# Attention and a 4-bit dense layer on one core: first queries in head order, and the second half's pieces of x split in the first stage

## The reference

```python
h = x + xattn(layernorm(x), ctx, ctx, pos, mask, Wq, Wk, Wv, Wo)   # x, ctx: (8, 256, 1024)
y = h + ffn(layernorm(h), qweight, qzeros, scales, bias)

def xattn(query, key, value, ...):    # 32 query heads, 8 key/value heads, head size 128
    q, k, v = heads(query @ Wq), heads(key @ Wk), heads(value @ Wv)
    q, k = rope(q), rope(k)           # q * cos + rotate_half(q) * sin
    scores = q k^T / sqrt(128);  where(mask == 0) -> -1e9
    return (softmax(scores) @ v) @ Wo

def ffn(x, ...):
    return x @ (scales * (w4 - zeros)) + bias   # w4: 4-bit values, 1024 x 1024
```

## Time and profile before

| | |
|---|---|
| Median of 3 runs | 2415.59 us (2408.92 to 2416.83) |
| Profiled execution, its own time | 2418.64 us |
| Its span, first to last instruction | 2416.8 us |
| Mean granted TensorE clock | 0.991 |
| PE busy | 2353.0 us, 97% |
| DVE, ACT, POOL busy | 1336.1, 1114.9, 1180.8 us |
| DMA | 346.65 MB, mean 143 GB/s |

### The profile page before, as it was taken

One profiled execution on the slowest core, in us unless ns is written; L12 is line 12 of the kernel. 1 busy time (PEld: TensorE's weight loads), 2 busy tenths in 40 slices (PEclk: granted clock), 3 DMA queues, 4 the chain that ended last, 5 costly groups with the idle time before them and its releaser, 6 DMA issues.

```text
span 2416.8 us, 33647 instructions
## 1 busy us (share of the span) xinstructions
PE 2353.0 (97%) x11552; PEld 1975.2 (82%) x11552; DVE 1336.1 (55%) x1949; ACT 1114.9 (46%) x2515; POOL 1180.8 (49%) x926
## 2 busy tenths in 40 slices
PE   8999998999999999899999999989999999999999
PEld 6887877888888888688888888868887877878887
DVE  4762554666666666666666666637743233343532
ACT  3222123667676667666766667643332222322010
POOL 1410535555665665556665566555664344355110
PEclk9999999999999999999999999999999999999999
DMA  7676674333434335343343333368554454443111
GB/s 262 237 178 223 233 246 152 92 102 100 113 103 114 105 106 155 113 127 102 93 117 106 106 112 103 111 212 284 202 191 168 149 178 166 143 177 113 44 44 53
DMA packets 201241, 346.65 MB, mean 143 GB/s; under 512 B 17744, under 2 KB 126544, under 8 KB 201168
## 3 DMA queue, kind: packets, MB, share of 16 engines
q1 hardware_dynamic: 187088, 310.06, 41.0%
q10 hardware_dynamic: 13312, 33.56, 4.2%
q0 software_dynamic: 768, 2.10, 0.3%
HBM read 238.69 MB, written 106.97 MB: 143 GB/s over the span
## 4 chain that ended last, share of the span: by engine, by line
PE 81%; DVE 7%; DMA 5%; ACT 3%; POOL 3%; issue 1%; SPq 1%; ACTq 0%; DVEq 0%; POOLq 0%
PE ps L208 18%; PE ps L209 18%; PE ps L210 18%; PE ps L690 7%; PE ps L691 7%; PE ps L692 7%; PE ps L622 4%; DMA scores<-in_ctx 2%; DVE rows L1226 1%; DMA xc_scratch<-xring 1%; DMA wraw<-in_L_xattn_Wo 1%; DMA xring<-in_x_tiles 1%; POOL s_buf L1322 1%; ACT probs L864 1%; PE ps L714 1%
## 5 line engine op out<-in xcount | busy, mean ns | idle before, releaser
L208 PE MATMUL ps<-act_t,wq_t 128*128 128x512 f32 x1280 | 512.5, 400 | 20.8 <-DVE act_t L1076 10.9
L210 PE MATMUL ps<-act_t,wq_t 128*128 128x512 f32 x1280 | 501.8, 392 | 0.0
L209 PE MATMUL ps<-act_t,wq_t 128*128 128x512 f32 x1280 | 501.6, 392 | 0.0
L690 PE MATMUL ps<-b_parts,a_parts 128*128 128x512 f32 x896 | 353.1, 394 | 11.3 <-POOL b_parts L1395 5.1
L1322 POOL TENSOR_TENSOR rope_tmp<-rope_tmp 128x512 f32<-128x512 f32 x144 | 192.4, 1336 | 341.8 <-DVE rope_tmp L1013 341.7
L691 PE MATMUL ps<-b_parts,a_parts 128*128 128x512 f32 x896 | 350.1, 391 | 0.0
L692 PE MATMUL ps<-b_parts,a_parts 128*128 128x512 f32 x896 | 349.7, 390 | 0.0
L1171 DVE TENSOR_TENSOR a_parts<-xring,a_parts 128x1024 fp32r<-128x1024 f32 x112 | 147.8, 1320 | 349.7 <-ACT a_parts L889 349.7
L1395 POOL TENSOR_TENSOR b_parts<-wraw,b_parts 128x512 fp32r<-128x512 f32 x112 | 195.7, 1748 | 275.1 <-ACT b_parts L894 275.1
L889 ACT ACTIVATE a_parts<-xring 128x1024 fp32r<-128x1024 f32 x112 | 118.7, 1060 | 415.8 <-PE ps L692 407.8
L208 PEld LDWEIGHTS ps<-act_t,wq_t 128*128 128x128 f32 x1280 | 242.5, 189 | 69.7 <-DVE act_t L1076 11.4
(11 more groups left out here) (111 smaller groups left out, 4437.8 us busy)
## 6 DMA issues: line engine op xcount, KB each, us to landing
xring<-left_scratch SPq DMA_DIRECT2D x112, 512.0 KB, 3.5
left_scratch<-s_buf SPq DMA_DIRECT2D x64, 640.0 KB, 5.3
wraw<-in_L_xattn_Wq SPq DMA_DIRECT2D x64, 512.0 KB, 4.0
wraw<-in_L_xattn_Wo SPq DMA_DIRECT2D x64, 512.0 KB, 4.4
v_scratch<-kv_t ACTq DMA_DIRECT2D x32, 512.0 KB, 3.0
k_scratch<-kv_t ACTq DMA_DIRECT2D x32, 512.0 KB, 5.1
kv_t<-k_scratch SPq DMA_DIRECT2D x64, 256.0 KB, 5.1
kv_t<-v_scratch SPq DMA_DIRECT2D x64, 256.0 KB, 4.6
```

The lines of the kernel that those rows point to most:

```text
L208: eng.matmul(dst, lh, rh, start=(k == first), stop=False)
L209: eng.matmul(dst, lh, rl, start=False, stop=False)
L210: mm = eng.matmul(dst, ll, rh, start=False, stop=(k == last))
L690: pe.matmul(dst, lh, rh, start=(begins and not onto), stop=False, skip_group_check=True)
```

## The change

The pieces are split in the first stage. In key units 3 to 10 ACT copies a centred piece into `probs_t[:, 0]` (`split_piece`) and DVE makes the rest in `probs_t[:, 1]` (`rest_of_piece`). SP stores both parts, 1 MB, and the next piece's load into an x buffer waits for the rest, no longer for the store. `split_piece(i)` waits for the store i - 1 to land. At the switch SP loads the two parts of each piece into their places, and PE waits for these loads; `piece_hi` and `piece_lo` are gone.

The first four query tiles are taken in the order `FIRST_TILES`: head 0 on both column tiles, then head 1. The wait for all of `x_lo` moves from the third to the second tile. The next weight's `head_hi` moves to after the first query on ACT, its `head_lo` to after the first query on POOL. The first unit's turn moves behind both halves of its query tile. An exponential of one column is added on ACT ahead of the first query.

```diff
+FIRST_TILES = ((0, 0), (0, 1), (1, 0), (1, 1))
+TILES = ((0, 0), (1, 0), (0, 1), (1, 1))
...
-        xc_dram = dram("xc_scratch", [8, P, 2, CT])
+        xc_dram = dram("xc_scratch", [8, P, 2, 2, CT])
...
             def load_piece(i):
                 if i < 2:
                     sp.wait_ge(ln_chain, 4 * TT)
                 else:
-                    sp.wait_ge(xc_stored, (i - 1) * 16)
+                    sp.wait_ge(piece_lo, i - 1)
...
             def store_piece(i):
-                sp.wait_ge(x_centred, i + 1)
-                sp.dma_start(xc_dram[i], x_pair[i % 2]).then_inc(xc_stored, 16)
+                sp.wait_ge(piece_lo, i + 1)
+                sp.dma_start(xc_dram[i], probs_t[:, :, :, :].bitcast(F32)).then_inc(xc_stored, 16)
...
             def load_tile(t):
                 if t < 2:
-                    sp.wait_ge(xc_stored, 8 * 16)
+                    sp.wait_ge(piece_lo, 8)
...
-                if 3 <= u < 11:
-                    store_piece(u - 3)
-                    if u - 1 < 8:
-                        load_piece(u - 1)
+                if 4 <= u < 12:
+                    if u - 2 < 8:
+                        load_piece(u - 2)
+                    store_piece(u - 4)
...
                         for k in range(4):
-                            sp.dma_start(act_v[:, 1, 2 * k:2 * k + 2, c * CT:(c + 1) * CT].bitcast(F32),
-                                         xc_dram[4 * c + k]).then_inc(xc_in[4 * c + k], 16)
+                            for l in range(2):
+                                sp.dma_start(act_v[:, l, 2 * k:2 * k + 2, c * CT:(c + 1) * CT].bitcast(F32),
+                                             xc_dram[4 * c + k, :, l, :, :]).then_inc(xc_in[4 * c + k], 16)
...
             def score(G, u8, first=False):
-                if b % 2 == 0:
+                if first:
+                    pe.wait_ge(q_lo, 3)
+                elif b % 2 == 0:
                     pe.wait_ge(q_lo, G * UPG + (4 * par + 2 * c + 2))
...
                     if switch and u8 in (4, 6):
-                        pe.wait_ge(x_lo, TT + 2 * (u8 - 4) + 2)
+                        for k in range(2):
+                            pe.wait_ge(xc_in[2 * (u8 - 4) + k], 32)
                     if more:
                         query(pair, i, 0, G * UPG + (u8 + 4))
-                    turn(G, u8, first=first and u8 == 0)
+                    if not (first and u8 == 0):
+                        turn(G, u8)
                     if switch and u8 in (4, 6):
-                        pe.wait_ge(x_lo, TT + 2 * (u8 - 4) + 4)
+                        for k in range(2, 4):
+                            pe.wait_ge(xc_in[2 * (u8 - 4) + k], 32)
                     if more:
                         query(pair, i, 1, G * UPG + (u8 + 4))
+                    if first and u8 == 0:
+                        turn(G, u8, first=True)
 
             pe.wait_ge(x_lo, TT // 2)
-            for i in range(4):
-                if i == 2:
+            for m, (j, c) in enumerate(FIRST_TILES):
+                if m == 1:
                     pe.wait_ge(x_lo, TT)
...
+            def split_piece(i):
+                act.wait_ge(x_centred, i + 1)
+                if i > 0:
+                    act.wait_ge(xc_stored, i * 16)
+                act.activation(probs_t[:, 0, :, :], x_pair[i % 2], ACT.Copy).then_inc(piece_hi, 1)
...
+                if 3 <= u < 11:
+                    split_piece(u - 3)
...
-            for m in range(3):
-                query_hi(0, 0, m, m)
+            act.wait_ge(ident_in, 16)
+            act.activation(row_sum[:, 0, 0, 0:1], identity[:, 0:1], ACT.Exp)
+            query_hi(0, FIRST_TILES[0], 0)
+            head_hi(0, 10 * 16, (q_done, 2))
+            query_hi(0, FIRST_TILES[1], 1)
+            query_hi(0, FIRST_TILES[2], 2)
             exponents(0, 0)
-            head_hi(0, 10 * 16, (q_done, 3))
             scaled(0, 0)
...
+            def rest_of_piece(i):
+                dve.wait_ge(piece_hi, i + 1)
+                dve.tensor_tensor(probs_t[:, 1, :, :], x_pair[i % 2], probs_t[:, 0, :, :].bitcast(F32),
+                                  ALU.subtract).then_inc(piece_lo, 1)
...
+                if 3 <= u < 11:
+                    rest_of_piece(u - 3)
...
             for m in range(3):
                 rope_sum(rope_tmp, q_rot, m + 1, q_sum)
-                query_lo(0, m, m)
-            head_lo(0, 19)
+                query_lo(0, FIRST_TILES[m], m)
+                if m == 0:
+                    head_lo(0, 19)
```

More of the change, by code:

```diff
@@ L186, in build @@
         x_centred, x_hi, x_lo, rope_scaled = sem("x_centred"), sem("x_hi"), sem("x_lo"), sem("rope_scaled")
+        piece_hi, piece_lo = sem("piece_hi"), sem("piece_lo")
         q_done, q_rot, q_sum, q_hi, q_lo = sem("q_done"), sem("q_rot"), sem("q_sum"), sem("q_hi"), sem("q_lo")
@@ L639, in attention @@
                     if switch and u8 in (4, 6):
-                        pe.wait_ge(x_lo, TT + 2 * (u8 - 4) + 2)
+                        for k in range(2):
+                            pe.wait_ge(xc_in[2 * (u8 - 4) + k], 32)
                     if more:
                         query(pair, i, 0, G * UPG + (u8 + 4))
-                    turn(G, u8, first=first and u8 == 0)
+                    if not (first and u8 == 0):
+                        turn(G, u8)
                     if switch and u8 in (4, 6):
-                        pe.wait_ge(x_lo, TT + 2 * (u8 - 4) + 4)
+                        for k in range(2, 4):
+                            pe.wait_ge(xc_in[2 * (u8 - 4) + k], 32)
                     if more:
                         query(pair, i, 1, G * UPG + (u8 + 4))
+                    if first and u8 == 0:
+                        turn(G, u8, first=True)
             pe.wait_ge(x_lo, TT // 2)
-            for i in range(4):
-                if i == 2:
+            for m, (j, c) in enumerate(FIRST_TILES):
+                if m == 1:
                     pe.wait_ge(x_lo, TT)
-                j, c = i % 2, i // 2
-                if i < 2:
+                if c == 0:
                     pe.wait_ge(w_lo, 17 + j)
-                else:
-                    pe.wait_ge(q_rot, i - 1)
-                products(pe, ps[:, BK_Q + j, :], lambda k: [wq_t[:, j, k, l, :] for l in range(2)],
+                if m >= 2:
+                    pe.wait_ge(q_rot, m - 1)
+                products(pe, ps[:, BK_Q + m % 2, :], lambda k: [wq_t[:, j, k, l, :] for l in range(2)],
                          lambda k: [act_v[:, l, k, c * CT:(c + 1) * CT] for l in range(2)],
@@ L851, in _, with query_hi @@
             store_unit(UNITS_A - 1)
-            def query_hi(G, par, i, m):
-                j, c = i % 2, i // 2
+            def query_hi(par, tile, m):
+                j, c = tile
                 act.wait_ge(q_sum, m + 1)
@@ L906, in attention @@
                     if not (last and u8 >= 5):
-                        query_hi(G, (u8 + 3) // 4 % 2, (u8 + 3) % 4, G * UPG + (u8 + 3))
+                        query_hi((u8 + 3) // 4 % 2, TILES[(u8 + 3) % 4], G * UPG + (u8 + 3))
                     if u8 < UPG - 1:
@@ L921, in attention @@
                         head_hi(0, G * 32 + (u8 // 4 * 16 + 11 * 16), (q_done, G * UPG + (u8 + 4)))
-                    if switch and u8 in (3, 4, 5, 6):
-                        piece_hi(2 * u8 - 5)
                     for kt in range(2):
@@ L928, in attention @@
                         act.activation(probs_t[:, kt, 0, :], ps[:, BK_T + kt, :], ACT.Copy).then_inc(pt_hi, 1)
-                    if switch and u8 in (2, 3, 4, 5):
-                        piece_hi(2 * u8 - 4)
                     if last and u8 in (5, 6):
@@ L934, in attention @@
                         scaled(nG, nxt)
-            for m in range(3):
-                query_hi(0, 0, m, m)
+            act.wait_ge(ident_in, 16)
[4 more added lines that the diff above has]
+            query_hi(0, FIRST_TILES[2], 2)
             exponents(0, 0)
-            head_hi(0, 10 * 16, (q_done, 3))
             scaled(0, 0)
             act.wait_ge(rope_stored, 32)
+            act.wait_ge(xc_stored, 8 * 16)
             attention(0, first=True)
@@ L1141, in _, with query_rot @@
                 tile_lo(t)
-            def query_rot(i, m, first=False):
-                j, c = i % 2, i // 2
+            def query_rot(bank, c, m, first=False):
                 dve.wait_ge(q_done, m + 1)
@@ L1148, in query_rot @@
                     dve.wait_ge(q_lo, m)
-                rotate(rope_tmp, BK_Q + j, c, q_rot)
+                rotate(rope_tmp, BK_Q + bank, c, q_rot)
             def masked(G, u8, half):
@@ L1178, in attention @@
                             dve.wait_ge(rope_in[(u8 - 5) // 2], 32)
-                        query_rot((u8 + 3) % 4, G * UPG + (u8 + 3))
+                        query_rot((u8 + 3) % 2, TILES[(u8 + 3) % 4][1], G * UPG + (u8 + 3))
                     if u8 < UPG - 1:
@@ L1185, in attention @@
                         masked(nG, nxt, nh)
```

(15 more changed lines are left out.)

## The result

The changed kernel takes 2424.09 us (median of 10 runs), the kernel before in the same jobs 2416.74. The ratio of the runs is 1.0034 with a 95% interval of 1.0025 to 1.0043: slower by 6 to 10 us. The profiled executions differ by 5.4 us of span, 2422.2 against 2416.8.

A forecast was written before the change was run, and what follows sets the result against it. PE, busy for 97% of the span, was taken as the bound. First stage +26.8, first queries -1.1 and switch -16.9 gave +8.8 us on a median of 2415.6: 2424, range 2409 to 2437.

The forecast's parts named there:

- wrong if: Signs against the forecast: stores landing under 6.9 us, PE waiting for `xc_in` loads, first query's wait 5 us or more.
- Switch, -16.9: At the switch: piece copies and subtractions leave ACT and DVE, PE waits for loads alone; a gain of 16.9 us.
- First stage, +26.8: Key units 3 to 11, second half: splitting and storing pieces holds the engines and delays unit 14; loss 26.8 us.
- the landings set the pace: First stage, likeliest case: store landings of 6.9 to 8.9 us set the period; 2421 to 2436, likeliest 2424; chance 0.50.
- L + 2.73: First stage's period per piece: store landing L, taken as 7.3 us, plus 2.73 for issues, ACT's half, DVE's rest.
- The floor, rival 3: First stage: store off the path, engines' waits on each other set 7.75 us per unit; loss 10.5, 2408; chance 0.13.
- First queries, -1.1: First four query tiles: PE waits 2.1 us before the second tile, yet the new order gains 1.1 us net.
- Rival 2: First stage: landings of 5.5 to 6.8 us, loss 14 to 23, sum -4 to +5, 2412 to 2421; chance 0.30.
- Rival 4: Switch: 4 MB arrive late, so the gain there is 3 us and the time 2438; chance 0.07.
- the two about waits at the switch and for POOL's weight: PE's waits: none on `act_t` at the switch, none for POOL's `wq_t`.
- the store per 10.0 us: First stage, SP: one piece store every 10.0 us, the last issued near 347.
- the waits of 9 us: First stage: PE waiting about 9 us before units 10, 12 and 14.

The follow-up runs named there:

- two_buffers: Changed kernel with a second buffer for the parts of a piece, so ACT waits for the store before the last; ratio 1.0019 to the kernel before.
- split_first_early: Changed kernel with two part buffers, ACT's half ahead of key copy, DVE's rest ahead of weight's, two x tiles loaded early; 2401.01 us, ratio 0.9944.

## Why the prediction was right, and where its steps were wrong

The time was forecast at 2424 and measured at 2424.09, slower by 8.8 us forecast and 6 to 10 measured. That owes much to errors that cancel, and the last digit to luck: the forecast added 8.8 to a base of 2415.6, while the kernel before has a median of 2416.74 over the ten runs, and the medians differ by 7.35. Two of the three signs that the forecast had named as "wrong if" came: the stores landed in 6.5 us, under 6.9, and PE's wait before the second query tile was 5.1.

- **Switch, -16.9: right**, in size and in cause. The eight loads per column tile were covered.
- **First stage, +26.8: measured +21.2.** The step that failed is "the landings set the pace". The landing was sized at 7.3 us and took 6.5: with it, the forecast's own L + 2.73 gives 9.2 per piece, which is what the units without a weight took (rests ending at 275.8 and 285.0). The units with a weight took 10.2 to 10.3 and were not set by the landing but by DVE, whose weight subtraction took 2.5 us beside POOL's centring. The last piece took 6.7 instead of 10.0, since the store before it had no load ahead and landed in 3.8. With L = 6.5 the forecast's own sum gives 21.1, nearly the 21.2 measured; that is luck, for it is some 1 us too low in each of three units and 2.5 too high in the last.
- **The floor, rival 3.** The forecast put the ring of engines at 7.75 us per unit and a loss of 10.5. `two_buffers` shows 9.15 per unit and 18.2 of stage. The size was off by the long subtractions, which the earlier trace rows had shown (1.79 us at 273.19 where 1.23 is usual) and the sum had passed over. With POOL's centring cut, the pair took 15.7 us (7.75 twice is 15.5) and the stage's loss was 10.0, near the forecast's 10.5: the floor was summed rightly for a ring without this collision. The stage's 21.5 us are thus 10.0 of plain ring, 8.2 of the collision and 3.3 of the landing, taken away in the order landing, collision.
- **First queries, -1.1: measured +1.1.** The step: PE's last wait before unit 14 was taken as 9 us long, so that the lower clock would hold PE back by 3.2 and shrink its wait for the tiles to 2.1 us. That wait was 2.07 us, since the last piece was quick (6.7 us) and PE ran its units 12 and 13 partly at the lower clock. PE came at full pace, waited 5.1 us and had the lower clock after it. The waits foreseen behind it came as said: 1.7 us before the first score, 1.0 and 1.2 in unit 1.
- **Rival 2** (landings from 5.5 to 6.8) named the measured landing. At 6.5 its sum is +3.1, on the profiled pair 2.3 too low, nearly all of it by the first queries. The fit cited for it in the prediction is given in the Trainium skill (DMA: Bandwidth & Descriptors, Anatomy of one DMA) for transfers issued by GpSimd, while SP issues these. Its estimate of 5.6 us was met by one of the six stores with a load ahead (5.7); the others took 6.4 to 6.6.
- **Rival 4** was wrong: no wait for the loads at the switch.
- Of the signs named, the two about waits at the switch and for POOL's weight held; the store per 10.0 us was one per 8.5 to 10.7, the last issued at 340.8; the waits of 9 us were 4.1, 6.5, 6.3 and 2.1.

Against the profiled pair (+5.4) the forecast of +8.8 is 3.4 too much: 5.6 too much in the stage, less 2.2 in the queries. The timed runs stand nearer to the forecast than the profiled pair does; a single execution differs from another by more than that (2421.2 to 2427.5 in ten runs).

## What to carry to other kernels

Work moved out of a stage that waits costs what it does to the order on each in-order engine where it lands: follow the ring (here DVE's rotation, POOL's sum, ACT's copy, ACT's half, DVE's rest, the next rotation) and put the moved step where its input is long ready, ahead of the instruction that waits; the same work then cost, with two buffers, 6 us of stage instead of 21. A second buffer helps at most as far as the traced waits for the first one go, and less where the freed steps run into another engine's: here it gave 3.3 us of 8.7. So look at what an instruction will stand beside once it comes earlier. Before a step is delayed, look at what it releases: a rest one unit later meant a load one unit later, and a stall of 9.7 us on a third engine.

## What the runs showed of the hardware

A DVE subtraction of 128x1024 from two SBUF operands took 1.21 to 1.23 us. In the pieces' units it took longer whenever a POOL operation on SBUF (the sum of 128x512 or the subtraction of 128x1024) had begun before it and still ran: 1.8 to 2.6 us in `two_buffers`, 1.7 to 3.4 in `split_first_early`. In each of these cases it ended 1.08 to 1.10 us after POOL's operation, however early it had begun, as in the rows of `two_buffers` above. So it seems to have done its work only then. With POOL's operation cut to 8 columns of each 512 all of DVE's in the pieces' units took 1.23. The other way round it is the same: where DVE's had begun first, POOL's subtraction took 2.7 to 3.4 us instead of 2.4 and ended 2.2 to 2.3 us after DVE's (`split_first_early`). The Trainium skill (SBUF — State Buffer, Terms) says this of the port pair shared by DVE and GpSimd: one of the two holds it for the whole of its instruction, and the other is fully blocked meanwhile. The trace agrees.

The common beginning of these kernels does not take the same time twice: DVE's first rotation of the last key units came between 246.4 and 251.4 us in the twelve profiled executions, whose instructions up to there do the same work. Two single executions' spans can therefore differ by 5 us for no other reason, and can't place a small effect; a stretch between two instructions places it better.
